# A modulated attention and FP6 block on one core: another prologue (order of loads, spread rows, weights from the grid, group 2's slots), and a rounded mask product

## The reference

```python
mod = (silu(c) @ wmod).reshape(8, 6, 1, 512)      # sa, ca, ga, sb, cb, gb
ga, gb = (2*(g >= 0) - 1) * maximum(abs(g), 0.25) for both gates
h = layernorm(x) * (1 + ca) + sa
x = x + ga * attention(h)
h = layernorm(x) * (1 + cb) + sb
x = x + gb * (mxquant(h) @ mxquant(weight).T + bias)
```

## Time and profile before

| | |
|---|---|
| median of 3 runs | 360.75 us (359.95 to 361.19) |
| the profiled execution | 359.63 us |
| its span | 357.7 us |
| mean granted TensorE clock | 0.967 of 2.4 GHz |
| busy: TensorE matmul, weight load | 318.3 us, 239.5 us |
| busy: VectorE, ScalarE, GpSimd | 283.9, 239.6, 234.0 us |
| moved by DMA | 68.5 MB, 191 GB/s over the span |

### The profile page before, as it was taken

One profiled execution on the slowest core, in us unless ns is written; L12 is line 12 of the kernel. 1 busy time (PEld: TensorE's weight loads), 2 busy tenths in 40 slices (PEclk: granted clock), 3 DMA queues, 4 the chain that ended last, 5 costly groups with the idle time before them and its releaser, 6 DMA issues.

```text
span 357.7 us, 6252 instructions
## 1 busy us (share of the span) xinstructions
PE 318.3 (89%) x2226; PEld 239.5 (67%) x2226; DVE 283.9 (79%) x499; ACT 239.6 (67%) x537; POOL 234.0 (65%) x139
## 2 busy tenths in 40 slices
PE   3788399878999989998999999978999989997894
PEld 1223266667898776786788678856887868675683
DVE  4994887965837997879898869797878889989932
ACT  3257566483978798689788889795779797241410
POOL 2063929059886896989599979994999399801000
PEclk9999589989999999999999999999899999998998
DMA  7997999973697097968598969497839791111122
GB/s 192 406 376 269 358 239 230 341 211 133 117 218 197 6 239 195 232 169 193 178 245 264 238 116 304 149 231 134 287 130 143 200 212 69 54 41 78 65 113 88
DMA packets 23797, 68.51 MB, mean 191 GB/s; under 512 B 2467, under 2 KB 2596, under 8 KB 19798
## 3 DMA queue, kind: packets, MB, share of 16 engines
q1 hardware_dynamic: 16224, 53.40, 44.3%
q0 software_dynamic: 7392, 14.68, 25.2%
q10 hardware_dynamic: 150, 0.02, 0.1%
HBM read 50.96 MB, written 17.14 MB: 190 GB/s over the span
## 4 chain that ended last, share of the span: by engine, by line
PE 42%; DVE 27%; ACT 12%; issue 7%; DMA 5%; POOL 4%; SPq 2%; DVEq 0%; ACTq 0%; POOLq 0%
PE ps L734 8%; PE ps L739 8%; PE ps L735 8%; DMA X<-in_wmod 5%; PE ps L717 4%; DVE Q L1200 4%; DVE amax L1181 4%; DVE DD L1207 3%; ACT U L490 3%; DVE XL L1157 3%; DVE X L1214 2%; ACT XH L458 2%; PE ps L645 2%; PE ps L820 2%; ACT unused L503 2%
## 5 line engine op out<-in xcount | busy, mean ns | idle before, releaser
L734 PE MATMUL ps<-WH,XH 128*128 128x512 f32 x256 | 108.4, 423 | 6.4 <-DVE X L1214 5.1
L735 PE MATMUL ps<-WL,XH 128*128 128x512 f32 x256 | 102.9, 402 | 0.0
L383 POOL TENSOR_TENSOR U<-U,c_bc 128x1024 f32<-128x1024 f32 x31 | 76.6, 2472 | 28.2 <-ACT U L490 28.1
L390 POOL TENSOR_TENSOR U<-U,sb_bc 128x1024 f32<-128x1024 f32 x31 | 74.2, 2394 | 4.8 <-POOL U L383 0.6
L1157 DVE TENSOR_TENSOR XL<-ps,XH 128x512 fp32r<-128x512 f32 x64 | 43.9, 686 | 38.2 <-ACT XH L458 38.1
L739 PE MATMUL ps<-WH,XL 128*128 128x512 f32 x256 | 70.6, 398 | 0.0
L458 ACT ACTIVATE XH<-ps 128x512 fp32r<-128x512 f32 x64 | 37.6, 587 | 48.6 <-PE ps L717 48.4
L490 ACT ACTIVATE U<-X,nmr,rstd 128x512 f32<-128x512 f32 x64 | 48.3, 808 | 30.7 <-DVE nmr L1174 28.1
L734 PEld LDWEIGHTS ps<-WH,XH 128*128 128x128 f32 x256 | 49.4, 193 | 17.9 <-DVE X L1214 6.8
L739 PEld LDWEIGHTS ps<-WH,XL 128*128 128x128 f32 x256 | 49.6, 194 | 11.2
L735 PEld LDWEIGHTS ps<-WL,XH 128*128 128x128 f32 x256 | 49.6, 194 | 8.8
(11 more groups left out here) (224 smaller groups left out, 426.5 us busy)
## 6 DMA issues: line engine op xcount, KB each, us to landing
X<-in_x SPq DMA_DIRECT2D x16, 1024.0 KB, 9.1
out<-X SPq DMA_DIRECT2D x15, 1024.0 KB, 5.5
X<-mod_scratch POOLq DMA_DIRECT2D x14, 1024.0 KB, 13.4
X<-in_wmod SPq DMA_DIRECT2D x2, 1024.0 KB, 14.7
sb_bc<-mod_scratch SPq DMA_DIRECT2D x7, 256.0 KB, 9.8
c_bc<-mod_scratch SPq DMA_DIRECT2D x7, 256.0 KB, 9.7
gb_bc<-mod_scratch SPq DMA_DIRECT2D x6, 256.0 KB, 7.8
X<-in_wmod SPq DMA_DIRECT2D x2, 512.0 KB, 4.4
```

Of the source, the lines that this page charges most:

```text
L383: nc.gpsimd.tensor_tensor(a, a, spread(c_bc[:, b % 2, :]), ALU.mult).then_inc(u_done, 2 if g == 0 else 1)
L390: nc.gpsimd.tensor_tensor(a, a, spread(sb_bc[:, b % 2, :]), ALU.add).then_inc(h_done, 2 if g == 0 else 1)
L734: M(bank, XH[:, n % 2, r], WH[:, b % 2, k, :], start=k == 0, stop=False)
L735: M(bank, XH[:, n % 2, r], WL[:, b % 2, k, :], start=False, stop=False)
```

## The change

- SyncE loads the columns of cb before w, those of gb and sb after it, then x of groups 1 and 2, and ca and sa without waiting for `columns_cp`. The stores of C's rows and of the columns follow each other behind that wait; x of group 4 follows SB's rows.
- TensorE starts with nine products of the array `ones` (128 x 128 float32), whose result nobody reads. C's eight rows are formed and spread over the partitions ahead of gb's rows. SB's row of batch 0 is formed on all partitions directly (`spread(3, ...)`, four 128 x 512 products), with gb's columns turned after the first of them; the eight rows of SB come after the turning of the weight.
- VectorE takes the weight to the grid only; GpSimd takes both halves back (`weights_from_grid`). VectorE adds V to the first half of group 0 only, GpSimd adds it to the second half, and to the halves of group 1 behind the scaled weight and behind `sum_by_dma(2)`. `bias_rows` comes after `first_v`, and `first_modulate` reads PSUM once TensorE has written it.
- Group 2's `SUM`, `DEVIATE` and `NORMAL` are one slot later. `deviations(1, 0)` moves behind tile 1's `high_part`.
- The mask operands are rounded to float32r by a cast of 2 x 640 on VectorE in slot 1 (`masks_row`), and the product takes them in that type.
- In iteration 1 VectorE scales in place in PSUM, copies the result to SBUF, and takes the difference with one operand in PSUM.

```diff
-        NORMAL = {2: (3, 3), 3: (6, 6), 4: (8, 9)}
-        DEVIATE = {2: (2, 2), 3: (5, 5), 4: (7, 7)}
-        SUM = {2: (1, 1), 3: (4, 4), 4: (5, 6)}
+        NORMAL = {2: (4, 4), 3: (6, 6), 4: (8, 9)}
+        DEVIATE = {2: (3, 3), 3: (5, 5), 4: (7, 7)}
+        SUM = {2: (2, 2), 3: (4, 4), 4: (5, 6)}
...
             load_x(0)
+            load_mod(2)
             sp.dma_start(Wd[:], w.rearrange("(c p) k -> p c k", p=P)).then_inc(w_in, 16)
             load_mod(1)
+            load_mod(3)
             load_x(1)
-            load_mod(2)
-            load_mod(3)
             load_x(2)
+            load_mod(4)
+            load_mod(5)
             sp.wait_ge(columns_cp, 1)
             sp.dma_start(mod_dram[0:COLUMNS].rearrange("w b d -> (w b) d"), column_rows).then_inc(columns_out, 16)
-            load_mod(4)
-            load_mod(5)
+            sp.dma_start(mod_dram[C], c_rows_all).then_inc(cs_out, 16)
...
+            def weights_from_grid(h):
+                pool.wait_ge(w_grid, h + 1)
+                a = blocks(Wd[:, HALF * h:HALF * (h + 1), :])
+                nc.gpsimd.tensor_tensor(a, blocks(Q8[:, h]), s32[:, h, :].unsqueeze(2).to_broadcast([P, HALF * NB, QB]),
+                                        ALU.mult).then_inc(wd_done, 1)
...
-            add_attn_bias(1)
-            scale_weights(0, Wfirst, 0, HALF)
-            scale_weights(0, Wfirst, HALF, NC)
+            add_attn_bias(0, 1)
+            weights_from_grid(0)
+            weights_from_grid(1)
+            scale_weights(0, Wfirst)
+            add_attn_bias(1, 0)
             modulate(0)
             sum_by_dma(2)
+            add_attn_bias(1, 1)
             scale_weights(1, Wsecond)
...
+            for k in range(UNTIL_LOADED):
+                M(ps[:, S_BANK, 0:P], ones[:], ones[:], start=True, stop=True)
...
             gate_columns(0)
+            rows_of(2, C_ROWS)
+
+            pe.wait_ge(rows_cp, 2)
+            M(ps[:, C_BANK, :], idf[0:B, 0:1].to_broadcast([B, P]), c_rows_all, start=True, stop=True).then_inc(cs_mm, 1)
             rows_of(1, GATE_ROWS)
+            spread(3, S_BANK, cs_mm, 0, 1)
             gate_columns(1)
-            rows_of(2, CS_ROWS)
+            spread(3, S_BANK, cs_mm, 1, NC)
...
-                    M(ba, mk[:, 0:P], mk[:, P:P + D], start=True, stop=False, skip_group_check=True)
+                    M(ba, mkr[:, 0:P], mkr[:, P:P + D], start=True, stop=False, skip_group_check=True)
...
                     if i == 1:
-                        TT(diff, cur[1], cur[0], ALU.subtract).then_inc(diff_done, 1)
+
+                        TT(held, held, scale, ALU.mult).then_inc(diff_done, 1)
                         dve.wait_ge(diff_done, 1)
+                        W_.tensor_copy(cur[1], bb).then_inc(ai_done, 1)
+                        TT(diff, bb, cur[0], ALU.subtract).then_inc(diff_done, 1)
...
             early_constants()
+            first_v()
             bias_rows()
-            first_v()
             dve.wait_ge(w_in, 16)
-            quantise(Wd[:, 0:HALF, :], Q8[:, 0], HALF * NB).then_inc(wd_done, 1)
+            weights_to_grid(0)
             gate(0, GA, BO, V, dve_step)
             chain[0] += 1
             dve.wait_ge(blq_mm, 1)
             W_.tensor_copy(aux[:, 0:1], blq_out).then_inc(blq_cp, 1)
+            weights_to_grid(1)
+            scales(0)
             gate(1, GB, BIAS, GBIAS, gb_col)
-            scales(0)
-            quantise(Wd[:, HALF:NC, :], Q8[:, 1], HALF * NB).then_inc(wd_done, 1)
             first_modulate()
```

More of the change, by code:

```diff
@@ L27 @@
 LAST = TILES * GROUPS
+UNTIL_LOADED = 9
 BEGIN, PERIOD = 9, 15
@@ L346, in spread, with add_attn_bias @@
                 return a.unsqueeze(1).to_broadcast([P, HALF, D])
-            def add_attn_bias(g):
+            def add_attn_bias(g, h):
                 pool.wait_ge(v_row, 1)
                 pool.wait_ge(x_in[g], 16)
-                for h in range(2):
-                    a = X1[:, g, HALF * h:HALF * (h + 1), :]
-                    nc.gpsimd.tensor_tensor(a, a, spread(v_bc[:]), ALU.add).then_inc(x1_done, 1)
+                a = X1[:, g, HALF * h:HALF * (h + 1), :]
+                nc.gpsimd.tensor_tensor(a, a, spread(v_bc[:]), ALU.add).then_inc(x1_done, 1)
+            def weights_from_grid(h):
[3 more added lines that the diff above has]
+                                        ALU.mult).then_inc(wd_done, 1)
             def sum_by_dma(g):
@@ L493, in sums @@
             def sums(g, h):
[L494 to L497, removed]
+                if g == 0 and h == 0:
+                    act.wait_ge(v_row, 2)
+                elif g < 2:
+                    act.wait_ge(x1_done, 2 * g + h)
                 else:
@@ L613, in _ @@
                 if q == 0:
-                    deviations(1, 1)
+                    for h in range(2):
+                        deviations(1, h)
                     for h in range(2):
@@ L627, in _, with spread @@
             M, TR = nc.tensor.matmul, nc.tensor.transpose
-            def spread_v():
-                for k in range(NC):
-                    pe.wait_ge(wmod_in[6 if k < HALF else 0], 16)
-                    m = M(ps[:, V_BANK, :], cE[:, k, 0:1].to_broadcast([P, P]), mod_w[0][:, k, :],
+            def spread(i, bank, signal, k0=0, k1=NC):
+                for k in range(k0, k1):
+                    pe.wait_ge(wmod_in[6 if i == 0 and k < HALF else i], 16)
+                    m = M(ps[:, bank, :], cE[:, k, 0:1].to_broadcast([P, P]), mod_w[i][:, k, :],
                           start=k == 0, stop=k == NC - 1)
-                m.then_inc(ga_mm, 1)
-            def spread(rows, bank, n, signal):
-                pe.wait_ge(rows_cp, n)
-                M(ps[:, bank, :], idf[0:B, 0:1].to_broadcast([B, P]), rows, start=True, stop=True).then_inc(signal, 1)
+                if k1 == NC:
+                    m.then_inc(signal, 1)
+            pe.wait_ge(cleared, 3)
+            for k in range(UNTIL_LOADED):
+                M(ps[:, S_BANK, 0:P], ones[:], ones[:], start=True, stop=True)
             def rows_of(i, bank):
@@ L681, in _ @@
             pe.wait_ge(silu_done, 1)
-            spread_v()
+            spread(0, V_BANK, ga_mm)
             rows_of(0, GATE_ROWS)
-            pe.wait_ge(cleared, 3)
             pe.wait_ge(rows_ok, 2)
@@ L920, in quantise_scales, with quantise, weights_to_grid @@
                 link(REC(inverse, scale))
-            def quantise_values(src, q8, nblk):
-                scale, inverse = (own[:, n:n + nblk] for n in (224, 256))
-                blk, q = blocks(src), blocks(q8)
-                link(TT(q, blk, wide(inverse), ALU.mult, saturate=False))
-                return TT(blk, q, wide(scale), ALU.mult)
+                return inverse
+            def quantise(src, q8, nblk):
+                scale = own[:, 224:224 + nblk]
+                inverse = grid_scales(src, scale, nblk)
+                link(TT(blocks(q8), blocks(src), wide(inverse), ALU.mult, saturate=False))
+                return TT(blocks(src), blocks(q8), wide(scale), ALU.mult)
+            def weights_to_grid(h):
+                a = Wd[:, HALF * h:HALF * (h + 1), :]
+                inverse = grid_scales(a, s32[:, h, :], HALF * NB)
+                TT(blocks(Q8[:, h]), blocks(a), wide(inverse), ALU.mult, saturate=False).then_inc(w_grid, 1)
             def temperatures():
@@ L964, in first_v @@
                 dve.wait_ge(x_in[0], 16)
-                for h in range(2):
-                    a = X1[:, 0, HALF * h:HALF * (h + 1), :]
-                    TT(a, a, v_bc[:].unsqueeze(1).to_broadcast([P, HALF, D]), ALU.add).then_inc(v_row, 1)
+                a = X1[:, 0, 0:HALF, :]
+                TT(a, a, v_bc[:].unsqueeze(1).to_broadcast([P, HALF, D]), ALU.add).then_inc(v_row, 1)
             def gate_bias_rows():
@@ L1107, in head_work @@
                     moments(xs[:], 0)
+                elif q == 1:
+                    masks_row()
                 elif q == 2:
```

91 lines of the change are left out of this document (44 added, 47 removed).

## The result

The changed kernel takes 358.84 us (median of 18 runs, 358.09 to 360.56) beside 360.99 us for the kernel before, run in turn with it. Some executions fall into a slower state; the ratio of the others is 0.9952 with a 95% interval of 0.9939 to 0.9965: **1.7 us faster**, between 1.3 and 2.2 (the two medians stand 2.15 apart). The forecast was 4.1 us less, 356.6; its range reached to 359.5 and held the time, its size did not come.

The account below looks back on a forecast made before the run. TensorE was taken to bound the steady part, load order the prologue. Group 1 3.4, masks' cast -0.6, mask products 1.9, copy -0.6: 4.1 off 359.63, 355.5; the median 1.1 higher, 356.6 us against 360.75; range 354.2 to 359.5.

Parts of the forecast that it names:

- The walk to group 1: Prologue up to GpSimd's start of group 1: 48.4 us instead of 51.78, 3.4 us gained.
- this outcome (2.4 for 2.8): First add of V: were VectorE blocked by GpSimd, `bias_rows` would end at 18.3 and the prologue give 2.4, not 2.8.
- between 0 and 0.8, and I take 0.6: Cost of the masks' cast, 640 columns on VectorE in slot 1, behind the maxima.
- That makes product 6 start at 77.9, while product 7 waits for group 2's data until 87.6. Nearly 2 us are left there: ScalarE's slot 4 delays XH of tile 6, yet product 7 still waits for group 2's data, with nearly 2 us left.
- The rival of a colder TensorE: Low clock after idling slows the products behind the weight's turning and product 0: end pays 0 to 1.5, 357.6; chance 0.14.
- cost nothing: TensorE's warm-up products at the start run before the first columns land, so they cost nothing.
- VectorE then waits for w: Prologue: the warm-up products can bring V's row 2 us earlier, but VectorE then waits for w, landing at 17.9.
- Masks and copy: Three mask products in float32r gain 0.65 each, 1.9 in all; iteration 1's extra VectorE operation costs 0.6.
- That rival, which needed 24: w, loaded third, lands late and moves group 1; with 24 us the time is 362.8; chance 0.07.
- the rival of the vanished gain: Slots above the fill are tighter and the prologue's gain goes; masks and copy leave 1.3, so 359.4; chance 0.09.
- "same": Outcome class of a change under 0.3% (1.1 us): 359.7 to 361.8 us.

Follow-up runs that it names:

- e1: The changed kernel with the cast of the masks moved from slot 1 to VectorE's prologue, where GpSimd is idle: 356.48 us, ratio 0.9881 to the kernel before.
- e11: The changed kernel with the cast of the masks moved from slot 1 to slot 2, where GpSimd is idle: 356.98 us, ratio 0.9905.
- the fillers: Products of ones keeping TensorE busy while it waits, in e7, e9 and e10: 357.75, 356.84 and 357.08 us.
- e12: Cast early, no copy in iteration 1, and without TensorE's nine products at the start: 357.27 us, ratio 0.9919.
- e6: e1 with the bias rows ahead of V's row, as in the kernel before: 357.16 us, ratio 0.9881.
- e9: e1 without the copy in iteration 1, plus 14 products of ones in TensorE's idle stretch behind product 5: 356.84 us, ratio 0.9903.
- e3: e1 with group 2's sums, deviations and normalising back in slots 1 to 3: 357.63 us, ratio 0.9906.
- e7: e1 plus products of ones in TensorE's idle stretches, 13 before group 1's transposes and 14 behind product 5: 357.75 us, ratio 0.9899.
- e4: The kernel before with only the mask product in float32r, cast in VectorE's prologue: 358.9 us, ratio 0.9949.
- e10: e1 without the copy, group 2's stages back in slots 1 to 3, and 15 products of ones before product 7: 357.08 us, ratio 0.9901.

## Why the prediction was wrong

- **The walk to group 1 was right** in its stations, 2.9 for 3.4. The missing 0.5 is the bias rows' cast beside GpSimd's add (w's reader at 18.38 for 17.9). The prediction had named this outcome (2.4 for 2.8) and put it aside by the earlier trace rows. That row shows a pair in which VectorE started first; it says who pays in that order, and nothing of the next VectorE instruction, which finds GpSimd at work.
- **The step that failed is the cast of the masks: "between 0 and 0.8, and I take 0.6".** It took 2.15 and cost 1.93 on VectorE's path, beyond its own bound, which came from a duration alone: the wait for GpSimd's L397, at work since 0.5 us before, had no term. With the cast in the prologue (e1) or one slot later (e11) the time is 356.5 and 357.0, about the forecast. That is in part luck: e1 gains 1.8 at product 7, not 2.8; 1.0 at product 41, net of the copy, less 1.0 up to 49 had no term either.
- **"That makes product 6 start at 77.9, while product 7 waits for group 2's data until 87.6. Nearly 2 us are left there"** also failed. Group 2's data was on time in e1 (ready at 87.5, 2.9 earlier than before; L421, `L414` before, 2.8 earlier), and so was XH of tile 6 (77.13 to 77.7). But TensorE went on at 79.24 and not at 77.9: VectorE's XL and WL, 1.3 us, stand between. Then, cold after 3.57 us of idle time, it took 5.24 us to product 6's last matmul, 3.64 before. The head's products behind it, which the prediction does not name, fit into its "nearly 2": by the kernel before, 3.9 for product 6, 3.6 for the head and 0.4 for what stands between lead from 77.9 to 85.8. The 1.3 and the 1.6 use up these 1.8, and TensorE takes the data up at 88.72, 1.1 behind the forecast and 1.8 earlier than before; the fillers gave 1.0 of it back. The rival of a colder TensorE named the mechanism, and 0 to 1.5 for its price, but put it at the turned weight and product 0, which ran at the full clock (1.00 over 34 to 41 us, 0.74 before).
- **The nine products "cost nothing": right; "VectorE then waits for w": wrong.** VectorE came to w 1.7 us behind its landing in the changed kernel, 0.2 in e1, 4.5 in e12; only in e6, with the bias rows first, did it wait. So they bring about 2.6.
- **Masks and copy were right:** 1.9 for three mask products, 0.6 for the copy. Nothing was forecast of the 1.6 us at product 41 and the 1.0 us up to product 49, of opposite signs.
- **w was not late:** it landed at 16.6 in the changed kernel and at 16.5 to 18.5 in the twelve profiles with this order of loads, 17.9 forecast. That rival, which needed 24, is out.
- **One count does not fit:** the rival of the vanished gain, 359.4, goes half to "same", but lies below the prediction's own bound of 359.7 for that.

The sum as it stands in the profiles: 0.1 at product 7, 1.9 by the masks, 1.0 from product 35 to 42 (1.6 less the copy's 0.6), less 1.0 up to product 49 and 0.9 up to 63: 1.1, which is the difference of the two profiled executions. The ratio of all runs gives more, 1.7.

## What to carry to other kernels

Before a VectorE instruction that copies or casts in SBUF, or reads SBUF twice, is put into a slot, look at what GpSimd runs at that moment: behind a GpSimd instruction of 2.4 us it costs the rest of that instruction and 0.3 to 0.7 more, in a place where GpSimd waits it costs its own 0.5. When you read the price of such a pair from a row, read also who started first. And where an idle stretch of TensorE moves, count the products at the low clock behind it, and everything queued between them and the next data.

## What was not expected of the hardware

- Even a cast over 2 partitions, 640 columns, waits for GpSimd: 2.15 us beside it, 0.48 alone; one over a single partition, 512 columns, 2.57 and 0.41.
- TensorE's nine small products at the start (4.2 us of its time) shorten the first eight steps with data from 5.71 to 6.67 us (three profiles without them) to 3.67 to 4.31 (ten with), and by that carry a prologue; in an eleventh, e9's, they do not (5.87).
- In e3's, e6's and e7's profile TensorE falls to the low level while it works on cb's columns (5.25 to 5.30 us for 3.60) and group 1 comes 0.8 to 1.0 us later than in e1 (49.03); in e4's it does so on gb's (5.13).
- Where TensorE falls to the low level later on differs from execution to execution: product 41 loses 1.6 us in the kernel before, e7 and e10, product 59 0.9 in the changed one and five others; none of this is in the code that was changed. Effects under 1 us can't be read from one profile's end, only from the stretch where they arise.
- Once TensorE stood for 3.65 us in the middle of a product with nothing to wait for (e7). Why is open.
